# Gated cross-attention on one core: the start of the schedule is put in another order

## The reference

```python
h = x + tanh(g_xattn[0]) * attn(ctx, ctx, layernorm(x))   # values, keys from ctx; queries from layernorm(x)
# attn: v = ctx @ Wv + bv; k = ctx @ Wk + bk; q = layernorm(x) @ Wq + bq; energy = q k^T
#       energy = where(mask == 0, most negative float, energy); softmax(energy / 4) v @ Wo + bo
out = h + tanh(g_ffn[0]) * tanh(layernorm(h) @ W1 @ W2 @ W3 + b_ffn)
```

## Time and profile before

| what | value |
|---|---|
| median of 3 runs | 1144.06 us (1143.8 to 1145.5) |
| time of the profiled execution | 1143.8 us |
| its span, first to last instruction | 1142.0 us |
| TensorE busy | 1096.7 us, 96% |
| VectorE, ScalarE, GpSimd busy | 85%, 70%, 69% |
| mean granted TensorE clock | 0.987 |

### The profile page before, as it was taken

One profiled execution on the slowest core, in us unless ns is written; L12 is line 12 of the kernel. 1 busy time (PEld: TensorE's weight loads), 2 busy tenths in 40 slices (PEclk: granted clock), 3 DMA queues, 4 the chain that ended last, 5 costly groups with the idle time before them and its releaser, 6 DMA issues.

```text
span 1142.0 us, 45478 instructions
## 1 busy us (share of the span) xinstructions
PE 1096.7 (96%) x19231; PEld 964.3 (84%) x19231; DVE 974.6 (85%) x1271; ACT 793.9 (70%) x1217; POOL 787.6 (69%) x1181
## 2 busy tenths in 40 slices
PE   7889999999999999999999999999999999999974
PEld 6768888888888888888888888888888888888764
DVE  6778888888888888889889888888888888888774
ACT  4466777677777767767767777776776777777641
POOL 5044777777777777777777777777777777777752
PEclk9999999999999999999999999999999999999996
DMA  6023333333343433333334344343333434433231
GB/s 173 30 85 107 106 108 112 115 115 106 118 129 88 131 116 111 110 115 116 105 115 119 101 126 122 89 132 115 115 106 115 117 103 124 123 88 115 87 99 63
DMA packets 109034, 124.76 MB, mean 109 GB/s; under 512 B 24353, under 2 KB 76066, under 8 KB 108834
## 3 DMA queue, kind: packets, MB, share of 16 engines
q1 hardware_dynamic: 108834, 121.86, 35.7%
HBM read 70.46 MB, written 51.38 MB: 107 GB/s over the span
## 4 chain that ended last, share of the span: by engine, by line
PE 92%; DVE 3%; issue 2%; DMA 1%; POOL 1%; ACT 1%; SPq 0%; POOLq 0%; DVEq 0%; ACTq 0%
PE ps_m L438 25%; PE ps_m L431 17%; PE ps_s L547 12%; PE ps_s L520 12%; PE ps_x L559 11%; PE ps_m L425 8%; PE ps_s L526 4%; PE ps_x L537 2%; DVE probs L911 1%; DMA scratch_a<-a_den 0%; PE ps_m L572 0%; DMA ctx_in<-in_ctx 0%; DVE neg_max L900 0%; POOL yn L331 0%; DMA den<-scratch_a 0%
## 5 line engine op out<-in xcount | busy, mean ns | idle before, releaser
L911 DVE TENSOR_TENSOR probs<-ps_s,far_T 128x2048 f32<-128x2048 f32 x128 | 292.6, 2286 | 28.3 <-PE ps_s L547 28.1
L900 DVE TENSOR_REDUCE neg_max<-ps_s 128x16 f32<-128x2048 f32 x128 | 292.1, 2282 | 6.0 <-PE ps_s L526 6.0
L722 ACT ACTIVATE probs<-probs 128x2048 f32<-128x2048 f32 x128 | 244.6, 1911 | 8.7 <-DVE probs L911 8.5
L697 ACT ACTIVATE q_aug<-ps_m,q_bias,q_scale 128x256 f32<-128x256 f32 x256 | 123.8, 565 | 140.3 <-PE ps_m L431 127.5
L370 POOL TENSOR_SCALAR th<-th,tgates 128x512 f32<-128x512 f32 x58 | 91.0, 1568 | 115.6 <-ACT th L738 115.6
L520 PE MATMUL ps_s<-k_aug,q_aug 32*128 32x128 f32 x4096 | 151.5, 284 | 10.6 <-DVE probs L911 10.4
L520 PEld LDWEIGHTS ps_s<-k_aug,q_aug 32*128 32x128 f32 x4096 | 127.2, 187 | 32.4 <-issue 32.4
L547 PE MATMUL ps_s<-q_aug,k_aug 32*128 32x128 f32 x4096 | 150.6, 283 | 2.2 <-DVE q_aug L906 1.2
L906 DVE TENSOR_TENSOR q_aug<-q_aug,ps_x 128x512 f32<-128x512 f32 x128 | 87.9, 686 | 67.3 <-PE ps_x L537 67.3
L547 PEld LDWEIGHTS ps_s<-q_aug,k_aug 32*128 32x128 f32 x4096 | 126.1, 186 | 21.7 <-issue 11.5
L559 PE MATMUL ps_x<-probs,v_ones 128*32 128x128 f32 x4096 | 140.1, 277 | 3.6 <-issue 1.9
(11 more groups left out here) (115 smaller groups left out, 1884.0 us busy)
## 6 DMA issues: line engine op xcount, KB each, us to landing
scratch_a<-a_den SPq DMA_DIRECT2D x64, 512.0 KB, 2.8
x_in<-in_x SPq DMA_DIRECT2D x64, 256.0 KB, 4.7
ctx_in<-in_ctx SPq DMA_DIRECT2D x64, 256.0 KB, 4.5
a_rows<-scratch_a SPq DMA_DIRECT2D x64, 256.0 KB
den_wide<-scratch_r SPq DMA_DIRECT2D x64, 256.0 KB
out<-y SPq DMA_DIRECT2D x64, 256.0 KB, 4.3
den<-scratch_a SPq DMA_DIRECT2D x64, 16.0 KB
scratch_r<-den_r SPq DMA_DIRECT2D x64, 16.0 KB, 1.4
```

Source lines behind the costliest of these rows:

```text
L697: last = nc.scalar.activation(dst[:, :, 2 * m + a, :], src[:, m * TOK:(m + 1) * TOK].rearrange("p (n q) -> p n q", q=P), ACT.Identity, bia ...
L722: nc.scalar.activation(tile, tile, ACT.Exp).then_inc(probs_ready, 1)
L900: nc.vector.tensor_reduce(out_v, ps_s[:], AX.X, ALU.max, negate=True).then_inc(max_ready, 1)
L911: nc.vector.tensor_tensor(probs[i % 2][:].rearrange("p j s q -> p (j s) q"), ps_s[:].rearrange("p j s q -> p (j s) q"), far_T[:].unsqueeze ...
```

## The change

The prologues are shortened and reordered.

- TensorE: `make_q(0)` is done ahead of `make_v(0)`, which goes to ps_m[2] and not to ps_x. The transpose of `far` stands between them. `turn_ctx(1)` and `turn_x(1)` move from the prologue to step 0 of the loop, behind `scores(0)`.
- TensorE, steps 0 to 3 of the loop: `make_q(t + 1)` and `make_k(t + 1)` stand behind `scores_T(i - 1)`, as in all later steps.
- ScalarE: `spread_q(0)` ahead of `keep_v(0)`; `high_of_ctx(1)` and `high_of_x(1)` move into step 0.
- VectorE: `setup_biases` moves ahead of `low_of_ctx(0)` and `rest(wk_s, ...)`; `moments_of_x(2)` moves into step 0, and `low_of_ctx(1)` and `low_of_x(1)` move behind `maxima(0)` there.
- Some waits move with their instructions, and a wait of VectorE on its own semaphore `stat1_ready` goes.

No instruction is added or removed, and SyncE's and GpSimd's programs stay as they are.

```diff
@@ -102,10 +102,8 @@
         BANK = {"xT": 0, "k": 0, "cT": 1, "q": 1, "v": 1, "yT": 0, "o": 2, "f": 2}
 
         def bank(name, p):
-            if (p, name) in ((0, "xT"), (1, "cT")):
+            if p == 0 and name in ("xT", "v"):
                 return ps_m[2]
-            if p == 0 and name == "v":
-                return ps_x[:].rearrange("p s q -> p (s q)")
             if p >= NP - 3 and name == "o" or p == NP - 1 and name == "yT":
                 return ps_m[1]
             return ps_m[0 if p == NP - 1 and name == "f" else BANK[name]]
@@ -441,7 +439,7 @@
 
             def turn_ctx(p):
                 if p == 1:
-                    pe.wait_ge(xT_ready, 1)
+                    pe.wait_ge(q_ready, 1)
                 if p > 1:
                     pe.wait_ge(v_ready, p)
                 pe.wait_ge(ctx_landed[p % 2], 16 * (p // 2 + 1))
@@ -473,8 +471,6 @@
             def make_q(p):
                 if p == 0:
                     pe.wait_ge(wq_ready, 1)
-                if p == 1:
-                    pe.wait_ge(q_ready, 1)
                 pe.wait_ge(cT_ready, p + 1)
                 pe.wait_ge(xT_ready, p + 1)
                 project_T(bank("q", p), wq_s, xT).then_inc(q_done, 1)
@@ -482,6 +478,7 @@
             def make_v(p):
                 if p == 0:
                     pe.wait_ge(wv_ready, 1)
+                    pe.wait_ge(xT_ready, 1)
                 if p > 0:
                     pe.wait_ge(q_ready, p + 1)
                 project(bank("v", p), cT, wv_s).then_inc(v_done, 1)
@@ -530,8 +527,6 @@
 
             def turn_max(i):
                 pe.wait_ge(max_ready, i + 1)
-                if i == 0:
-                    pe.wait_ge(farT_ready, 1)
                 wait(pe, a_ready, i - 2 if i < NB - 1 else i - 1)
                 for a in range(2):
                     last = nc.tensor.transpose(ps_x[:, a, :], neg_max[i % 2][:, a * D:a * D + P], ident[:])
@@ -603,13 +598,11 @@
             turn_ctx(0)
             make_k(0)
             turn_x(0)
-            make_v(0)
             make_q(0)
-            turn_ctx(1)
-            pe.wait_ge(v_ready, 1)
             pe.wait_ge(far_ready, 1)
             nc.tensor.transpose(ps_x[:, 0, :], far[:], ident[:]).then_inc(far_turned, 1)
-            turn_x(1)
+            make_v(0)
+            pe.wait_ge(farT_ready, 1)
             for t in range(NP):
                 for half in range(2):
                     i = 2 * t + half
@@ -626,17 +619,16 @@
                             make_o(t - 4)
                         if is_pair(t - 5):
                             turn_y(t - 5)
-                        if t < 4:
-
-                            make_q(t + 1)
-                            make_k(t + 1)
+                        if t == 0:
+                            turn_ctx(1)
+                            turn_x(1)
                     else:
                         if is_pair(t + 1):
                             make_v(t + 1)
                     if is_batch(i - 1):
                         scores_T(i - 1)
                     if half == 0:
-                        if t >= 4 and is_pair(t + 1):
+                        if is_pair(t + 1):
                             make_q(t + 1)
                             make_k(t + 1)
                     else:
@@ -748,10 +740,8 @@
             high_of_x(0)
             act.wait_ge(biases_ready, 1)
             spread_k(0)
+            spread_q(0)
             keep_v(0)
-            spread_q(0)
-            high_of_ctx(1)
-            high_of_x(1)
             act.wait_ge(gates_landed, 16 * 2)
             nc.scalar.activation(tgates[:], gates[:], ACT.Tanh).then_inc(gates_ready, 1)
             for t in range(NP):
@@ -763,6 +753,9 @@
                     tanh(t - 6)
                 if is_pair(t - 5):
                     high_of_y(t - 5)
+                if t == 0:
+                    high_of_ctx(1)
+                    high_of_x(1)
                 if is_pair(t + 1):
                     spread_q(t + 1)
                 if is_batch(2 * t - 1):
@@ -890,7 +883,6 @@
             def moments_of_x(p):
                 dve.wait_ge(x_landed[p % X_RING], 16 * (p // X_RING + 1))
                 wait(dve, ln_step, RSTD * (p - 1))
-                wait(dve, stat1_ready, p)
                 moments(0, x_in[p % X_RING], stat2[p % 2], stat1_ready)
 
             def maxima(i):
@@ -978,27 +970,29 @@
                 nc.vector.memset(stat2[i][:].rearrange("p a b c -> p (a b c)"), 1.0)
             setup_spreads()
             moments_of_x(0)
+            setup_biases()
             low_of_ctx(0)
             rest(wk_s, wk_raw, w_high, 1, wk_ready)
-            setup_biases()
             rest(wq_s, wq_raw, w_high, 2, wq_ready)
             rest(wv_s, wv_raw, w_high, 3, wv_ready)
             moments_of_x(1)
             low_of_x(0)
             setup_mask()
-            moments_of_x(2)
-            low_of_ctx(1)
-            low_of_x(1)
             keep_far()
             dve.wait_ge(zeros_ready, 2)
             for t in range(NP):
                 if is_batch(2 * t - 1):
                     append_max(2 * t - 1)
+                if t == 0:
+                    moments_of_x(2)
                 if t > 0 and is_pair(t + 1):
                     low_of_ctx(t + 1)
                     low_of_x(t + 1)
                 if is_batch(2 * t):
                     maxima(2 * t)
+                if t == 0:
+                    low_of_ctx(1)
+                    low_of_x(1)
                 if is_pair(t - 4):
                     add_residual(t - 4)
                 if is_pair(t - 5):
```

## The result

The changed kernel takes 1156.92 us (median; 1155.46 to 1158.41) against 1144.32 us for the kernel before on the same chip. The ratio is 1.0118, with a 95% interval of 1.0102 to 1.0136: slower by 12.6 us. I had said 1153.0 us and a range up to 1156.3, so the direction was right and the time lies above the range. The profiled execution took 1157.39 us, with a span of 1155.6 us, 13.6 more than the span of 1142.0 before.

The account below looks back on a forecast made before the run. TensorE was taken to bound the kernel, so any lateness at step 4 stays to the end. +1.0 + 3.55 + 1.9 + 2.5 = +9.0 us on 1143.8 gave 1152.8, stated as 1153.0 us; range 1147.5 to 1156.3.

Parts of the forecast that it names:

- What bounds the kernel: Whole body: TensorE busy 956.59 of 960 us, so the change only moves the moment at which the body begins.
- Part 1: Prologue up to `scores(0)`: VectorE waits for the bias column's DMA, delaying k(0) and q(0); +1.0 us, bounds -0.4 and +2.4.
- Part 2: Step 0: pair 1's preparation loses its cover and its remainders wait behind `maxima(0)`; q(1) 3.55 us later.
- Part 3: Steps 1 to 3: the stall moves from before `scores` to before `scores_T`, which waits for the reduction; +1.9 us.
- Part 4: Granted clock: new idle times in steps 0 to 3 bring slow stretches of 5.5 us, two old ones vanish; net +2.5 us.
- Rival 1: Prologue: the bias wait is not on the path, -0.4 and not +1.0 us, 1151.6 us; chance 0.08.
- rival 2: Steps 0 to 3: the clock does not fall after the new idle times; +3.4 us, 1147.5 us; chance 0.11.
- rival 3: Steps 1 to 3: earlier reductions make the wait of `scores_T` cost nothing; faster, 1140.9 us; chance 0.03.
- rival 4: Body: idle time there absorbs the late start, so no change; 1144 us; chance 0.04.

Follow-up runs that it names:

- after_again: The changed kernel run once more, unchanged: 1158.3 us, ratio 1.0116 to the kernel before.
- a_bias: Changed kernel with VectorE's bias setup put back behind the remainder of Wk: 1154.82 us, ratio 1.0097.
- a_step0: Changed kernel with pair 1's remainders on VectorE ahead of the first reduction in step 0: 1154.77 us, ratio 1.0092.
- b_again: The kernel before run once more, unchanged: 1141.46 us (one run).
- a_fill: Changed kernel with q computed twice in steps 1 to 3, as useless work in the idle time before the transposed scores: 1151.84 us, ratio 1.0059.
- a_loop: Changed kernel with q and k ahead of the transposed scores again in steps 0 to 3: 1153.07 us, ratio 1.0076.
- b_split: Kernel before with q ahead of the transposed scores and k behind them in steps 1 to 3: 1142.89 us, ratio 0.9981.
- b_again2: The kernel before run another time, unchanged, as a control: 1146.56 us, ratio 1.0006.
- b_bias: Kernel before with only VectorE's bias setup moved ahead of ctx(0)'s remainder: 1146.45 us, ratio 1.0007.
- a_all: Changed kernel with bias setup back, pair 1's remainders ahead of step 0's reduction, and q and k split around the transposed scores: 1147.4 us, ratio 1.0008.

## Why the prediction came out too low

- **What bounds the kernel**: right. The body is 999.2 us before and 999.6 after, and within 998.1 to 1001.0 in all fourteen profiles.
- **Part 1, +1.0 us**: right in its mechanism and, at full clock, in its size: after_again has `scores(0)` at 17.74, forecast 17.84. Its bound of 1.4 us for the lower clock came true in the first profile (19.52), together with a column that landed 0.4 us later. a_bias shows that the cause is the wait.
- **Part 2, +3.55 us**: right in its sum. q(1) starts 5.28 us behind `scores(0)`, forecast 5.36, with 2.72 us of idle, forecast 2.7. a_step0 shows that the reduction is on that path, but it takes only 1.0 us off, where the bound had 2.3: 2.5 of the 3.5 us are the preparation of pair 1 itself, with its copies.
- **Part 3, +1.9 us**: right. Measured at full clock it is +1.8 (9.52, 11.15 and 9.97 us against 9.22, 9.61 and 9.99 in b_again; the first and third from a_fill, whose `scores_T` start as in the changed kernel, 4.7 us behind `scores(2)` and 5.6 behind `scores(6)`). 3.18, 2.20 and 2.20 us of idle as forecast, and none before `scores(3)`, `(5)`, `(7)`.
- **The sum of the order** can be checked without the clock: each interval of the changed kernel at full clock (q(1) 5.28 us behind `scores(0)` and 3.68 from there to `scores(1)`, as before; then 8.16; 9.52; 8.17; 11.15; 7.78; 9.97; 7.78) from 17.74 on puts `scores(8)` at 89.2. The kernel before without slow stretches is b_again, 83.0. That is +6.2 us, where parts 1 to 3 said +6.45.
- **Part 4, the clock, net +2.5 us**: this step failed, by its size. The changed kernel's mark lies 7.3 us above 89.2 in both profiles, where I had 5.5. The stretch behind 3.18 us of idle cost 2.6 and 1.5 us (I took 1.0), that of step 0 1.5 and 2.8 us (1.5), those of steps 2 and 3 together 1.5 and 3.0 us (3.0). In the first profile the prologue adds 1.8 us, 0.4 of it the late column; my sum had that slow stretch at nothing and only the bound had it. q(0), behind 1.50 us of idle, took 2.90 us in four of the seven profiles with this prologue order and 1.7 in three. And I subtracted 3.0 us for the two stretches of the kernel before as if every execution had them. Its mark is 3.0, 0 and 3.3 us behind that of b_again in three profiles, 2.1 on the mean (0.3 of the 3.3 arose before `scores(1)`). Net it is +5.2 and not +2.5.
- **The base**: I laid the whole sum on one execution, whose end of 56.8 us is the shortest of fourteen. The ends of the three profiles of before have a mean of 58.4 us, the two of the changed kernel 59.5 both: another 1.1 us. With two and three profiles, whether this is a draw or an effect of the change stays open; a_loop with 60.5 and a_fill with 57.8 us have the same end of the program and lie on both sides. All fourteen kernels have the same end; the seven built on the changed kernel have 59.5 us on the mean, the seven built on the kernel before 58.6, and each group spreads by 3 to 4 us. The clock is part of it: the granted clock of the end is 0.81 in b_again and b_split (57.7 and 57.9 us) and 0.70 to 0.76 in the four with more than 60 us. It isn't all: at 0.79 the end took 56.8 to 59.6 us.
- Together 6.2 + 5.2 + 1.1 = 12.5 us, and the medians differ by 12.6. These are means of three and two profiles, so that they meet to 0.1 us is in part luck.
- **The range** had room for slow stretches but only 0.5 us for what executions differ by. They differ by several microseconds in this kernel. By the account above, the clock's +5.2 lies inside its bound of +5.5, and the time passed the range with the end.
- **Rival 1** (bias wait off the path) is refuted by a_bias, **rival 2** (the clock does not fall) by the profile and a_fill, **rival 3** (earlier reductions) by the three idle times released by them, **rival 4** by the result. The rule of the Trainium skill ("TensorE: Matmul & The Clock Gate", Part 1 on oscillation) puts the danger at idle gaps longer than these, and the measurement goes against it: the clock fell behind 1.70, 2.14, 2.20 and 2.72 us.

## What to carry to other kernels

When an operation is moved behind another to remove a wait, look for the wait that it had covered: here 4.7 us of idle before the scores became 7.6 us before the transposed scores (1.0 of it had stood before q(2)), and the work that covers both waits was to be split between them. Where an engine's idle time brings the clock down, price it as a chance and over several profiles, above all for the kernel that one subtracts from. Nothing that waits for a DMA should be queued ahead of work on the path unless its landing time is well clear: the tiny operations on VectorE were 0.4 us of the price here, the wait in front of them the rest.

## What the runs showed of the hardware

- The same idle time of TensorE brings the granted clock to 0.50 in one execution and leaves it at 1.00 in another. Over the profiles: 1.70 us before `scores(3)`, in two of five executions (before and b_again2, not b_again, a_loop and b_bias); 2.14 us before `scores(7)`, in four of these five; 2.20 us, in eight of ten cases; 2.72 us in step 0, in four of five (not a_fill); 3.18 us, in five of five. An idle of 1.75 us in step 0 did so in a_all and not in a_step0. No idle up to 1.26 us had a slow stretch behind it, between 20 and 100 us.
- One slow stretch costs 1.4 to 1.6 us where TensorE is the bound, and 2.6 to 2.8 us where the low clock lasted longer (step 1 of the first profile, step 0 of after_again and a_bias).
- 36 useless matmuls in idle time made the stretch around them 4.0 us quicker, not slower (54.4 and not 58.4 us).
- One small DMA of a bias column (1 KB, issued at 3.25 to 3.27 us in the same place of the queue) let VectorE go on at 7.0 to 8.0 us.
- Twelve matmuls can take the 2.9 us of the lower clock in the first 20 us while the view by stretches shows a granted clock of 1.00 (k(0) and q(0) of the changed kernel).
